# Mixture of experts in a two-layer gated attention kernel: the first matrix once for both choices, both gelus mixed on VectorE, the second matrix once

## The reference, cut to what matters

```
probs = jax.nn.softmax(x @ W_r.T + b_r, axis=-1)
w_topk, idx_topk = jax.lax.top_k(probs, K)                 # K = 2
base1 = x @ W1.T + b1                                      # 256 -> 1024, the same for both choices
u1 = jnp.einsum('nd,erd->ner', x, A1)                      # E * R = 64 low-rank values
for k in range(K):
    oh = jax.nn.one_hot(idx_topk[:, k], E, dtype=x.dtype)
    z1 = (u1 * oh[:, :, None]).reshape(N, E * R)
    h = act(base1 + z1 @ B1_rf * SCALING)                  # gelu, SCALING = 2
    u2 = jnp.einsum('nf,erf->ner', h, A2)
    z2 = (u2 * oh[:, :, None]).reshape(N, E * R)
    y = h @ W2.T + b2 + z2 @ B2_rf * SCALING               # 1024 -> 256
    res = res + w_topk[:, k:k + 1] * y
```

## Time and profile before

| | |
|---|---|
| time, median of 3 runs (lowest to highest) | 7147.93 us (7139.51 to 7154.99) |
| the profiled execution's own time, and its span | 7151.02 us, 7149.2 us |
| busy over the span: PE, DVE, ACT, POOL | 85%, 79%, 61%, 52% |
| stages before `moe` | 0 to 5080.8 us |
| `moe`: layernorm and loads, turning and router | 5080.8 to 5142.0 us |
| `moe`: masks and turning of the low-rank values | 5142.0 to 5161.1 us |
| `moe`: main loop | 5161.1 to 5648.9 us |
| stages behind it | 5648.9 to 7149.2 us |

### The profile page before, as it was taken

The page is one execution under the profiler, slowest core; times in us unless marked ns, Lnnn a source line. Parts: engine busy times, 40 slices in busy tenths (PEclk is TensorE's granted clock), DMA queues, the critical chain, the costliest instruction groups (busy, mean ns, idle before and its releaser), DMA issues. The chain is left out here.

```text
span 7149.2 us, 180318 instructions
## 1 busy us (share of the span) xinstructions
PE 6052.2 (85%) x64319; PEld 2559.1 (36%) x64326; DVE 5668.0 (79%) x8927; ACT 4380.6 (61%) x4245; POOL 3730.7 (52%) x3972
## 2 busy tenths in 40 slices
PE   2761899999999999999999999999499667999623
PEld 2330133333333333333333333333355444544311
DVE  5885899999999999999999999999300346777655
ACT  0330089888898898888889888899000011666401
POOL 2331088888888888888888888888000001000000
PEclk7895599999999999999999999999688787999856
DMA  1432111001101101101100110110200058777500
GB/s 61 111 104 94 34 19 23 13 15 24 18 10 25 19 8 25 22 11 20 24 14 15 24 18 10 25 19 7 44 0 0 3 220 233 116 113 115 95 27 10
DMA packets 182696, 319.61 MB, mean 45 GB/s; under 512 B 97188, under 2 KB 143717, under 8 KB 176643
## 3 DMA queue, kind: packets, MB, share of 16 engines
q1 hardware_dynamic: 181784, 307.60, 20.2%
HBM read 196.26 MB, written 113.33 MB: 43 GB/s over the span
## 5 line engine op out<-in xcount | busy, mean ns | idle before, releaser
L1024 DVE TENSOR_REDUCE a_mx<-PS 128x1 f32<-128x512 f32 x6620 | 4073.0, 686 | 227.2 <-PE PS L908 223.6
L995 ACT ACTIVATE a_e<-PS,a_sk 126x1024 f32<-126x1024 f32 x3264 | 3630.2, 1113 | 459.2 <-PE PS L893 106.9
L771 POOL TENSOR_SCALAR a_p<-a_e 126x1024 f16<-126x1024 f32 x3264 | 3408.4, 1044 | 648.2 <-ACT a_e L995 596.1
L908 PE MATMUL PS<-a_K,a_Q 48*128 48x512 bf16 (+1 forms) x6884 | 2107.0, 383 | 49.9 <-DMA a_K<-d_inv 49.9
L893 PE MATMUL PS<-a_Q,a_K 54*126 54x512 bf16 x6528 | 2110.1, 404 | 27.7 <-issue 18.6
L935 PE MATMUL PS<-a_e,a_sel 126*32 126x256 f32 x26112 | 1992.8, 382 | 0.0
L893 PEld LDWEIGHTS PS<-a_Q,a_K 54*126 54x126 bf16 x6528 | 614.4, 131 | 1377.3 <-issue 1318.8
L931 PE MATMUL PS<-a_p,a_V 128*32 128x256 f16 x13056 | 959.6, 284 | 14.5 <-ACT a_og L976 10.5
L931 PEld LDWEIGHTS PS<-a_p,a_V 128*32 128x32 f16 x13056 | 336.7, 93 | 1250.2 <-POOL a_p L771 1054.2
L935 PEld LDWEIGHTS PS<-a_e,a_sel 126*32 126x32 f32 x26112 | 755.6, 110 | 8.5 <-issue 2.0
L1827 DVE TENSOR_REDUCE b_mx<-PS 128x1 f32<-128x512 f32 x803 | 504.7, 684 | 187.9 <-PE PS L1711 187.9
(11 more groups left out here) (288 smaller groups left out, 3717.1 us busy)
## 6 DMA issues: line engine op xcount, KB each, us to landing
b_K<-d_k SPq DMA_DIRECT2D x210, 200.1 KB, 6.0
a_K<-d_k SPq DMA_DIRECT2D x102, 400.2 KB
d_v<-v1v SPq DMA_DIRECT2D x9, 3328.0 KB, 11.5
b_V<-d_v SPq DMA_DIRECT2D x36, 832.0 KB, 12.0
d_k<-k_T SPq DMA_DIRECT2D x400, 63.0 KB, 1.7
d_k<-k1p SPq DMA_DIRECT2D x54, 400.2 KB, 7.6
a_V<-d_v SPq DMA_DIRECT2D x68, 204.0 KB, 2.8
d_v<-vq SPq DMA_DIRECT2D x17, 803.2 KB
```

The lines of the kernel that those rows point to most:

```text
L771: g.tensor_scalar(p[0:rows, kk % RE, :], e[0:rows, kk % RE, :], 1.0, SHIFT, ALU.mult, ALU.add).then_inc(rounded, 1)
L908: last = pe.matmul(self.PS[:, M_BANK + j % sh.SLOTS, c0:c0 + wd], Qb[M_ROWS, ii % 4, t * P:(t + 1) * P], Kb[M_ROWS, (ii // NC) % 2, k0:k0 ...
L995: a.activation(e[0:r, kk % RE, :], self.PS[0:r, e_bank(i, s):e_bank(i, s) + 2, :], ACT.Exp, scale=skb[0:r, hb, s:s + 1]).then_inc(exp_done, 1)
L1024: v.tensor_reduce(mx[:, col:col + 1], bank, AX.X, ALU.max).then_inc(max_done, 1)
```

## The change

Nothing outside `moe` is touched. Inside it:

- The loop runs over four chunks instead of eight units. For each f the two W1 matmuls and the B1 matmul of choice 0 are made once, ScalarE takes gelu 0, and then a second B1 matmul adds the difference z1(choice 1) - z1(choice 0) into the same bank (`second`), from which ScalarE takes gelu 1. Three banks rotate. B1 is loaded twice, on partitions 0 to 63 and 64 to 127, so choice 0 uses rows 0 to 63 of the array and the difference rows 64 to 127.
- u2 (`low_rank`) is made with A2 as the loaded weights and `hT` as 512 moving columns, choice 0 in array columns 0 to 63 and choice 1 in columns 64 to 127, so it comes out turned already. VectorE multiplies it by a turned mask `mT` that holds one-hot, factor 2 and weight (one instruction), and no turning is left in the loop.
- VectorE mixes the two gelus, `hc` = w0 * h0 + w1 * h1, three instructions of 128x512 for each f (`tmp`, `wb`); W2 is then applied once to `hc`, and B2, doubled over 128 rows, once to `z2T` (`mixed`).
- TensorE's order: hidden rows of chunk c + 1 stand ahead of the output of chunk c.
- Ahead of the loop the two pairs of blocks for z1 become part of the router block: masks for all experts at once, two turnings of 128 rows (low-rank values, masks), and eight matmuls with a matrix of sixteenths that spread the weights over all partitions (`wb`).
- The loads become 12 instead of 10 (B1 and B2 twice), the router's weights first.

The diff, cut to its core; of the removed lines, which stand in the function printed above, it shows only those of TensorE's hidden rows:

```diff
+                    pe.wait_ge(z_ready, 1)
+                    for t in range(NT):
+                        ins = pe.transpose(self.PS[:, 4 + t // 4, (t % 4) * P:(t % 4 + 1) * P], zm[:, t, 0:P], self.idf[:, :])
+                    ins.then_inc(turned, 1)
...
+                    pe.wait_ge(m_taken, 1)
+                    pe.wait_ge(z_taken, 2)
+                    pe.wait_ge(ranked, EXPERTS + 1)
+                    for c in range(NCH):
+                        for k in range(2):
+                            r = slice(k * ER, (k + 1) * ER)
+                            ins = pe.matmul(self.PS[:, 2 * c + k, :], part[r, :], mT[r, c * CH:(c + 1) * CH], start=True, stop=True)
+                        ins.then_inc(w_ready, 1)
...
+                    a.wait_ge(turned, 1)
+                    for i in range(2):
+                        a.activation(zT[:, i * 2 * CH:(i + 1) * 2 * CH], self.PS[:, 4 + 2 * i:6 + 2 * i, :].rearrange("p b n -> p (b n)"),
+                                     ACT.Copy).then_inc(z_taken, 1)
+                    for c in range(NCH):
+                        a.wait_ge(w_ready, c + 1)
+                        a.activation(wb[:, :, c * CH:(c + 1) * CH], self.PS[:, 2 * c:2 * c + 2, :], ACT.Copy)
...
+                    z = [zm[:, :, k * ER:(k + 1) * ER] for k in range(2)]
+                    mask = [zm[:, :, P + k * ER:P + (k + 1) * ER] for k in range(2)]
+                    for k in range(2):
+                        L(v.tensor_scalar(mask[k].rearrange("p t (e r) -> p t e r", r=RANK), along(oh[:, k, :, :], 3, RANK),
+                                          2.0, None, ALU.mult))
+                        L(v.tensor_tensor(z[k], psu, mask[k], ALU.mult))
+                    L(v.tensor_tensor(z[1], z[1], z[0], ALU.subtract))
+                    v.sem_inc(z_ready, 1)
+                    for k in range(2):
+                        L(v.tensor_tensor(mask[k], mask[k], along(wk[:, k, :], 2, ER), ALU.mult))
+                    v.sem_inc(m_ready, 1)
+                    L(v.tensor_tensor(wsum[:, :], wk[:, 0, :], wk[:, 1, :], ALU.add))
+                    v.wait_ge(turned, 2)
+                    L(v.tensor_copy(mT[:, :], self.PS[:, 0:4, :].rearrange("p b n -> p (b n)")))
+                    v.sem_inc(m_taken, 1)
...
+                    def second(c, f):
+
+                        m = c * NF + f
+                        pe.wait_ge(h_done[0], m + 1)
+                        pe.matmul(self.PS[:, m % 3, :], B1[ER:2 * ER, f * P:(f + 1) * P], zT[ER:2 * ER, tokens(c)],
+                                  start=False, stop=True, skip_group_check=True).then_inc(h_ready[1], 1)
+
+                    def hidden(c):
                         for f in range(NF):
-                            m = n * NF + f
-                            if m >= 2:
-                                pe.wait_ge(h_done, m - 1)
+                            m = c * NF + f
+                            if m >= 3:
+                                pe.wait_ge(h_done[1], m - 2)
                             for q in range(2):
-                                pe.matmul(self.PS[:, m % 2, :], W1[:, q, f * P:(f + 1) * P], xT[:, q, c * CH:(c + 1) * CH],
+                                pe.matmul(self.PS[:, m % 3, :], W1[:, q, f * P:(f + 1) * P], xT[:, q, tokens(c)],
                                           start=(q == 0), stop=False)
-                            pe.matmul(self.PS[:, m % 2, :], B1[:, f * P:(f + 1) * P], z1T[:, k, c * CH:(c + 1) * CH],
-                                      start=False, stop=True).then_inc(h_ready, 1)
-                        pe.wait_ge(h_done, (n + 1) * NF)
-                        if n >= 1:
-                            pe.wait_ge(y_taken, n)
+                            pe.matmul(self.PS[:, m % 3, :], B1[0:ER, f * P:(f + 1) * P], zT[0:ER, tokens(c)],
+                                      start=False, stop=True).then_inc(h_ready[0], 1)
+                            if f >= 1:
+                                second(c, f - 1)
+                        second(c, NF - 1)
+
...
+                    def low_rank(c):
+                        for k in range(2):
+                            pe.wait_ge(h_done[k], (c + 1) * NF)
+                        if c >= 1:
+                            pe.wait_ge(z_ready, c)
+                        for f in range(NF):
+                            for k in range(2):
+                                ins = pe.matmul(self.PS[k * ER:(k + 1) * ER, 3, :], A2[:, f, :], hT[:, c % 2, k, f, :], start=(f == 0),
+                                                stop=(f == NF - 1), tile_position=(0, k * ER), skip_group_check=True)
+                        ins.then_inc(u_ready, 1)
+
+                    def mixed(c):
+                        if c >= 2:
+                            pe.wait_ge(y_taken, c - 1)
+                        y = lambda t: self.PS[:, 4 + 2 * (c % 2) + t // 2, (t % 2) * D:(t % 2 + 1) * D]
+                        for f in range(NF):
+                            pe.wait_ge(hc_ready, c * NF + f + 1)
+                            for t in range(4):
+                                pe.matmul(y(t), hc[:, f, t * P:(t + 1) * P], W2[:, f, :], start=(f == 0 and t % 2 == 0), stop=False, skip_group_check=True)
+                        pe.wait_ge(z_ready, c + 1)
                         for t in range(4):
+                            ins = pe.matmul(y(t), z2T[:, t * P:(t + 1) * P], B2[:, :], start=False, stop=True, skip_group_check=True)
                         ins.then_inc(y_ready, 1)
+                    hidden(0)
+                    low_rank(0)
+                    for c in range(NCH):
+                        if c + 1 < NCH:
+                            hidden(c + 1)
+                        mixed(c)
+                        if c + 1 < NCH:
+                            low_rank(c + 1)
...
+                    def gelu(c, f, k):
+                        m = c * NF + f
+                        a.wait_ge(h_ready[k], m + 1)
+                        a.activation(hT[:, c % 2, k, f, :], self.PS[:, m % 3, :], ACT.Gelu_apprx_tanh,
+                                     bias=b1[:, f:f + 1]).then_inc(h_done[k], 1)
+                    for c in range(NCH):
+                        if c >= 2:
+                            a.wait_ge(u_ready, c - 1)
+                            a.wait_ge(hc_ready, (c - 1) * NF)
...
+                            gelu(c, f, 0)
+                            if f >= 1:
+                                gelu(c, f - 1, 1)
+                        gelu(c, NF - 1, 1)
...
+                    def out(c):
+                        v.wait_ge(y_ready, c + 1)
+                        for t in range(4):
+                            L(v.scalar_tensor_tensor(out=yt[:, t, :], in0=b2[:, :], scalar=wsum[:, 4 * c + t:4 * c + t + 1],
+                                                     in1=self.PS[:, 4 + 2 * (c % 2) + t // 2, (t % 2) * D:(t % 2 + 1) * D],
+                                                     op0=ALU.mult, op1=ALU.add))
+                        v.sem_inc(y_taken, 1)
+                        xs = self.x[:, 4 * c:4 * c + 4, :]
+                        L(v.scalar_tensor_tensor(out=xs, in0=yt[:, :, :], scalar=self.gates[:, 2:3], in1=xs,
+                                                 op0=ALU.mult, op1=ALU.add))
+                    for c in range(NCH):
+                        if c >= 1:
+                            v.wait_ge(y_ready, c)
+                        v.wait_ge(u_ready, c + 1)
+                        L(v.tensor_tensor(z2T[:, :], self.PS[:, 3, :], mT[:, tokens(c)], ALU.mult))
                         v.sem_inc(z_ready, 1)
+                        for f in range(NF):
+                            L(v.tensor_tensor(hc[:, f, :], hT[:, c % 2, 0, f, :], wb[:, 0, tokens(c)], ALU.mult))
+                            L(v.tensor_tensor(tmp[:, :], hT[:, c % 2, 1, f, :], wb[:, 1, tokens(c)], ALU.mult))
+                            L(v.tensor_tensor(hc[:, f, :], hc[:, f, :], tmp[:, :], ALU.add))
+                            v.sem_inc(hc_ready, 1)
+                        if c >= 1:
+                            out(c - 1)
+                    out(NCH - 1)
```

More of the change, by code:

```diff
@@ L1230, in moe @@
[L1230 to L1235, removed]
+            zT = self.sb(ctx, "z1T", [2 * ER, sh.T])
+            mT = self.sb(ctx, "maskT", [2 * ER, sh.T])
+            wb = self.sb(ctx, "w_rows", [P, 2, sh.T])
@@ L1251, in _ @@
                     for i in range(EXPERTS):
[L1252 to L1253 removed]
+                        g.memset(ranks[:, i:i + 1], float(EXPERTS - i)).then_inc(ranked, 1)
+                    g.memset(part[:, :], 1.0 / (2 * RANK)).then_inc(ranked, 1)
                 @block.scalar
@@ L1310, in moe @@
-            units = [(c, k) for c in range(sh.T // CH) for k in range(2)]
-            with ExitStack() as c2:
-                h_ready, h_done = self.sem(c2, "h_ready"), self.sem(c2, "h_gelu")
-                y_ready, z_ready, z_turned = self.sem(c2, "y_ready"), self.sem(c2, "z2_ready"), self.sem(c2, "z2_turned")
```

(32 more changed lines are left out.)

124 lines of the change are left out of this document (45 added, 79 removed).

## The result

| | before | after |
|---|---|---|
| time, median (lowest to highest) | 7151.46 us (7139.51 to 7155.49, 4 runs) | 6873.30 us (6863.75 to 6875.01, 4 runs) |
| the profiled execution: time, span | 7151.02, 7149.2 us | 6872.02, 6870.2 us |
| start of the last router step's last instruction | 5141.30 | 5142.19 us |
| from its end to the loop's first matmul | 19.6 us | 20.7 us |
| main loop, first matmul to last DVE instruction's end | 487.7 us | 207.6 us |

The ratio is 0.9611, 95% interval 0.9594 to 0.9628. The forecast was 6873.0 us. The table by stage of the changed kernel, in the columns of the earlier trace rows: the loop, the stretch ahead of it, the first u2, the second u2.

The account below looks back on a forecast made before the run. TensorE was taken to bound the main loop: 487.7 to 210.7 us, 277.0 less, with 2.3 more ahead of it, gives -274.7 us. The median 7147.9 us thus becomes 6873 us, range 6850 to 6910.

Parts of the forecast that it names:

- Halves side by side: B1 matmuls of choice 0 and the difference share the array; four passes cost 1.05 us, an f stays 2.97.
- the rival's f of 3.83 us: Row halves in a line: B1 passes cost 0.86 us more per f; 6900 us, chance 0.13 shared with column strips.
- three-slot rival: B1 pairs: lower half waits for upper half's second pass, 0.43 us more for 28 pairs; 6885 us, chance 0.16.
- Strips side by side: u2's 32 passes in two column strips take 16 slots, 7.1 us a chunk; in a line 14.0.
- Hidden chunk: Hidden rows of a chunk: eight f, 23.8 us, plus 1.9 for the last f's gelu wait and second B1: 25.7.
- Output: W2 and B2 matmuls of a chunk: 72 passes at 0.238 us, 17.1 us.
- Low clock: Start of the loop: the first f runs at a lower clock, 4.59 us against 2.97, adding 1.6 us.
- Last chunk: Behind the last u2, paced by DVE: 0.8 + 17.8, last f and B2 1.9 each, output 3.4; 25.8 us.
- The rival's low clock: Last chunk's passes at 1.2 GHz: eight take 3.4 us, 10 us later; 6883 us, within a shared chance of 0.10.
- Ahead of the loop: Last router step to first matmul: masks, turnings, spreading take 21.9 us, 2.3 more than now; range -1 to +6.
- Loads: Start of `moe`: two more load issues, 1.2 us, and 0.3 MB stay below 12.5 us of cover, costing nothing.
- Mixing hidden: z2T and mixing on DVE, 18.6 us a chunk, covered by the next chunk's 25.7 us hidden rows, except the last.

Follow-up runs that it names:

- before_gelu: The kernel before, with only three f of the next unit's hidden rows moved ahead of u2: 7100.64 us, ratio 0.9946 to the kernel before.

## Why the prediction was right

The two profiled executions differ by 279.0 us (7151.02 to 6872.02); the forecast had 274.7. Point by point:

- **TensorE bounds the loop.** Right: 195.5 of 207.7 us busy, no DVE wait in chunks 0 to 2.
- **Halves side by side**, given 0.48 along with the strips. Right by the rows above, and the experiment with both on the same rows gives the rival's f of 3.83 us. The three-slot rival (the lower half behind the upper half's second pass) is excluded by the common start at 5170.99.
- **Strips side by side.** Right, 7.09 us against 7.1; 12.3 to 14.0 with the strips apart.
- **Hidden chunk** 25.7 us. Right: from one u2's start to the next are 48.4 us, of which output and u2 take 22.8 and the hidden rows 25.6. The wait for f = 7's gelu, 0.77 us, is the 0.8 of the sum.
- **Output** 17.1 us a chunk: mis-sized, 15.7 measured (5224.14 to 5239.87), 0.218 us a pass. The 0.238 of the earlier trace rows came from a stretch with the passes of B2 on 64 rows between, and so with changes of form that the new output does not have. In three chunks 4.2 us less.
- **Low clock.** The first f took 2.94 us (5163.16 to 5166.10), as at full clock, 1.6 us less than the sum; instead the first u2 took 8.78 us, 1.7 more. That the two cancel is luck.
- **Last chunk** 25.8 us: 26.9 measured. From u2's end to the first mixing 1.0 us pass instead of 0.8, the 24 mixing instructions take 18.5 instead of 17.8 (2.29 us an f against 2.225, and one pause of 0.51 us), the end of the output 3.6 instead of 3.4. The rival's low clock did come, for the first f alone: its eight passes took 3.4 us (5347.15 to 5350.55), as the rival had it. But the next f ran at 0.22 us a pass, and by the fourth TensorE had caught up with DVE; from then on 8 passes take 1.99 us, with waits of 0.30. So it cost nothing.
- **The loop** 210.7 us: 207.6 measured, and -4.2 - 1.6 + 1.7 + 1.1 gives 207.7.
- **Ahead of the loop** 21.9 us: 20.7 measured, 1.1 more than before where 2.3 were forecast. The masks with one source take 0.69 us as the lower bound had it, and the spreading takes 5.25 us, in pairs:

```profile
5142.51 0.69 DVE L1321 TENSOR_SCALAR zm<-onehot 128x1024 f32<-128x1024 f32 x1
...
5156.44 5.25 PE L1270 MATMUL PS<-maskT,sixteenths 64*128 64x512 f32 x16 [2.52 <-DVEq L1332]
```

- **Loads** at nothing: right. From the layernorm's first instruction to the end of the last router step 60.8 us pass before (5080.80 to 5141.59) and 60.7 after (5081.78 to 5142.48). The 0.9 us by which that step ends later arose ahead of `moe`, and what lies behind the loop is 0.9 us shorter; executions of one kernel differ by more.
- **Mixing hidden** by the next chunk's hidden rows: right. In the kernel that has no chunk ahead it is exposed, 21.1 of the 28.8 us. The prediction's bound for a late DVE, 1.5 us an instruction, is 1.6 by its own numbers ((25.7 + 15.0 - 0.75 - 0.4) / 24, less the gap); nothing hangs on it.

Loop and ahead of it give -280.1 + 1.1 = -279.0, 4.3 us more gain than forecast. That the median came within 0.3 us of the forecast is chance: the forecast started from a median of 7147.93, which a fourth run moved to 7151.46.

What the prediction did not see: it counted the clock's return in u2 as part of u2's new form. The kernel before could have had 82 of the 280 us by order alone, and at least 52 of them were the clock. Of the rest, the runs size W1 once at 55 us, W2 once with mixing at 49, the halves at 19 and the strips at 21; these were taken out one at a time and need not add up. No run isolates what is left, some 54 us; by the rows, two u2 of 7.36 us becoming one of 7.09 in each of four chunks would be 31 of them, which is an estimate.

## What to carry to other kernels

Where TensorE sets the end, count its passes by the shortest clean row of each shape and sum them: W1 and W2 once came out within 1 us of that. Take a rate from a stretch with the same neighbours, since changes of form between matmuls are part of it. Before removing work at a low clock, look at the waits ahead of it: laying independent matmuls over them can return more than the waits themselves. And put the instructions that are to share the array next to each other.

## What the runs showed of the hardware

- Two float32 matmuls on rows 0 to 63 and 64 to 127 that write to different PSUM banks start within 0.01 us pass by pass, so that the first pass of the later matmul (L1353, 5170.99) starts ahead of the second of the earlier one (L1364, 5171.52). By their first starts and last ends the two matmuls stay in the program's order, 0.01 us apart.
- Strips with one strip's 16 passes all ahead of the other's overlap in about four passes at the seam: 12.29 us against 7.09.
- Waits of 0.8 us ahead of u2 cost more than themselves: 512 moving columns 8.78 against 7.09 us (clock 0.81 and 1.00), 64 moving columns 11.90 against 7.36 us (0.55 in the stretch of the earlier trace rows, 1.00 in `before_gelu`), although nothing of the work differs.
- A fallen clock need not cost time: in the last chunk eight passes took 3.4 us instead of 1.7 at a clock of 0.55, and TensorE made it up while DVE set the pace.
